# More lead in a shared FFN, spread weight loads, and a scatter that waits for its own transfers

## The reference

```python
scores = sigmoid(h @ gate_w.T)                 # 32 experts in 4 groups
topi   = top 8 of the 2 best groups            # per token
x_lat  = h @ fc1_w.T                           # 512 -> 256
y_lat  = sum over the 8 of cw * (relu(x_lat @ w1[e].T)**2 @ w2[e].T)
shared = relu(h @ shared_up_w.T)**2 @ shared_down_w.T    # 512 -> 1024 -> 512
out    = x + shared + y_lat @ fc2_w.T
```

## Time and profile before

| | us |
|---|---|
| median of 3 runs (lowest, highest) | 1316.29 (1312.57, 1317.66) |
| the profiled execution, its own time | 1316.76 |
| its span | 1314.9 |
| PE busy in the span | 1110.3 (84%) |
| POOL busy in the span | 595.5 (45%) |

### The profile page before, as it was taken

How to read it: one execution, slowest core, us unless ns; L and a number is a source line. 1 busy time by engine, 2 the same in 40 slices (tenths; PEclk the granted TensorE clock), 3 DMA queues, 4 the chain that set the end, 5 groups by cost and what they waited for, 6 DMA issues and landing times.

```text
span 1314.9 us, 14151 instructions
## 1 busy us (share of the span) xinstructions
PE 1110.3 (84%) x3686; PEld 651.0 (50%) x3687; DVE 735.5 (56%) x1387; ACT 461.2 (35%) x694; POOL 595.5 (45%) x461
## 2 busy tenths in 40 slices
PE   0374499997989899799899589996999999999928
PEld 0131244433433344354444234445888888888813
DVE  8574478989998999751683000003444444444425
ACT  3352256535653655241211011111333333333400
POOL 3223204641464147400037666621777777777720
PEclk9987799998999899899899789997999999999959
DMA  3969901002100201301108542236777777777684
GB/s 129 303 209 357 368 5 48 25 16 72 48 24 16 80 8 32 115 0 64 64 36 279 189 164 94 90 121 201 131 121 133 124 127 129 123 132 122 86 237 171
DMA packets 125731, 157.57 MB, mean 120 GB/s; under 512 B 8705, under 2 KB 103937, under 8 KB 125697
## 3 DMA queue, kind: packets, MB, share of 16 engines
q1 hardware_dynamic: 96512, 117.83, 29.2%
q0 software_dynamic: 29184, 39.34, 16.1%
HBM read 79.67 MB, written 77.46 MB: 120 GB/s over the span
## 4 chain that ended last, share of the span: by engine, by line
PE 55%; DVE 19%; another core or an unknown queue 6%; issue 6%; DMA 5%; SPq 4%; ACT 2%; POOL 1%; DVEq 0%; POOLq 0%; ACTq 0%
PE banks L561 11%; PE banks L582 11%; PE banks L490 8%; PE banks L1556 8%; PE banks L513 6%; DMA arena<-fT 4%; DVE arena L1336 3%; DVE arena L1433 3%; PE banks L551 3%; PE banks L572 3%; PE banks L1574 2%; PE banks L473 2%; DVE arena L1317 2%; DVE arena L1344 1%
## 5 line engine op out<-in xcount | busy, mean ns | idle before, releaser
L1556 PE MATMUL banks<-arena 128*128 128x512 f32 x896 | 390.4, 596 | 28.7 <-ACT arena L1092 18.9
L451 POOL DMA_INDIRECT sums<-arena x160 | 249.6, 1560 | 142.8 <-ACT arena L688 112.1
L1556 PEld LDWEIGHTS banks<-arena 128*128 128x128 f32 x896 | 171.3, 191 | 245.6 <-issue 225.3
L439 POOL DMA_INDIRECT slots_in<-arena x128 | 129.3, 1010 | 106.3 <-issue 86.4
L490 PE MATMUL banks<-arena 128*128 128x512 f32 x320 | 148.5, 611 | 16.2 <-ACT arena L659 13.3
L561 PE MATMUL banks<-arena 128*128 x640 | 153.0, 382 | 0.0
L582 PE MATMUL banks<-arena 128*128 x640 | 151.2, 379 | 0.0
L513 PE MATMUL banks<-arena 128*128 128x512 f32 x256 | 118.8, 608 | 8.8 <-DVE arena L894 7.1
L1574 PE MATMUL banks<-arena 128*128 128x512 f32 (+1 forms) x64 | 44.3, 856 | 96.7 <-DVE arena L1399 72.6
L561 PEld LDWEIGHTS banks<-arena 128*128 128x128 f32 x640 | 116.5, 192 | 13.2 <-issue 0.4
L843 DVE SCALAR_TENSOR_TENSOR arena<-arena 128x256 f32<-128x256 f32 x160 | 72.1, 490 | 89.2 <-ACT arena L673 89.2
(11 more groups left out here) (179 smaller groups left out, 1367.2 us busy)
## 6 DMA issues: line engine op xcount, KB each, us to landing
slots_in<-arena SPq DMA_DIRECT2D x8, 2800.0 KB, 18.4
arena<-slots_in SPq DMA_DIRECT2D x80, 280.0 KB, 3.3
sums<-arena SPq DMA_DIRECT2D x4, 2176.0 KB, 20.5
arena<-fT SPq DMA_DIRECT2D x32, 256.0 KB, 2.6
arena<-xT SPq DMA_DIRECT2D x8, 1024.0 KB, 5.5
arena<-w2T SPq DMA_DIRECT2D x4, 2048.0 KB
arena<-sums SPq DMA_DIRECT2D x16, 512.0 KB, 8.7
arena<-w1T SPq DMA_DIRECT2D x3, 2048.0 KB
```

The source lines that it names most:

```text
L439: pool.indirect_dma_start(rows_in, bass.IndirectOffsetOnAxis(ap=POSU[:, n, j:j + 1], axis=0), XLR[:, n], None).then_inc(S['scattered'], 16)
L451: pool.indirect_dma_start(sums[g % RING], bass.IndirectOffsetOnAxis(ap=DESTU[:, g:g + 1], axis=0), YO[:, i % 4, c], None, compute_op=ALU.add)\
L1556: ins = pe.matmul(out, w[:, k, m * P:(m + 1) * P], x[:, k], start=(k == 0), stop=(k == kt - 1))
```

## The change

Three edits go together.

- **Lead.** LAG = KS - 2 = 6: PE does `up(0)` to `up(5)`, `ranks()`, and then `up(n)`, `down(n-6)` alternately; at the end six `down` tiles stand together.
- **Gate and fc1 tiles.** AHEAD = EARLY - 3 = 9: tiles 9, 10 and 11 move from ahead of `k2` to behind `v2`, with banks 5, 6 and 3. Their logits and rows move behind the last sequence's sigmoid and `XS` on ACT and DVE. Waits on `rows_copied` and `logits_copied` move with them.
- **Loads and scatter.** W2's four quarters and the first three of W1 are issued one by one between `up_mm` 16 and 32. `xg_load` of the first four pairs now stands ahead of the last four W1 loads (its buffer is moved, so that it doesn't lie over `HS`), behind a wait for all of `scattered`. POOL drops the waits for `up_mm` and waits instead, after every second token tile (16 DMAs), until all issued so far have landed. PE's wait for W1 and W2 moves behind the first two transposes of the experts.

```diff
-            for e in range(0, E, quarter):
-                sp.dma_start(W2[:, e:e + quarter], w2[:, e:e + quarter]).then_inc(S['w2_loaded'], 16)
+            load_w2(0)
             sp.wait_ge(S['up_mm'], KS * 2)
-            load_w1(0)
+            load_w1(0, quarter)
+            load_w2(1)
+            sp.wait_ge(S['up_mm'], KS * 2 + KS // 2)
+            load_w2(2)
+            sp.wait_ge(S['up_mm'], KS * 3)
+            load_w1(quarter, quarter // 2)
+            load_w2(3)
             sp.wait_ge(S['up_mm'], KS * B)
-            load_w1(1)
-            load_w1(2)
+            load_w1(quarter + quarter // 2, quarter // 2)
+            load_w1(2 * quarter, quarter)
+            sp.wait_ge(S['scattered'], 16 * NT * TOPK)
+            for i in range(4):
+                xg_load(sp, i, i, 0)
             for k in range(0, KS, 2):
...
-            sp.wait_ge(S['scattered'], 16 * NT * TOPK)
-            for i in range(4):
-                xg_load(sp, i, i, 0)
...
                 for j in range(TOPK):
-                    g = (n * TOPK + j) // 4
-                    if j % 4 == 0:
-                        pool.wait_ge(S['up_mm'], 5 + 3 * g // 4)
                     pool.indirect_dma_start(rows_in, bass.IndirectOffsetOnAxis(ap=POSU[:, n, j:j + 1], axis=0),
                                             XLR[:, n], None).then_inc(S['scattered'], 16)
-            pool.wait_ge(S['scattered'], 16 * TOPK * NT)
+                if n % 2:
+                    pool.wait_ge(S['scattered'], 16 * TOPK * (n + 1))
...
+        LAG = KS - 2
+        def stream():
+            for n in range(KS * B + LAG):
+                if n < KS * B:
+                    yield 'up', n
+                if n >= LAG:
+                    yield 'down', n - LAG
...
+        AHEAD = EARLY - 3
+        FG_BANK = [(3, 4, 0, 1, 7, 2)[n % 6] if n < AHEAD else (5, 6, 3, 4, 7, 2, 5)[n - AHEAD] for n in range(NT)]
...
+                if n == AHEAD:
+                    pe.wait_ge(S['r2_evac'], 4 * B)
+                if n == NT - 1:
+                    pe.wait_ge(S['rows_copied'], AHEAD + 1)
+                    pe.wait_ge(S['logits_copied'], AHEAD + 1)
...
-            fg_tiles(pe, range(3, EARLY))
+            fg_tiles(pe, range(3, AHEAD))
...
-            pe.wait_ge(S['w1_loaded'], 16 * (3 + KS // 2))
-            pe.wait_ge(S['w2_loaded'], 64)
             pe.wait_ge(S['routed'], 2)
             pe.wait_ge(S['down_evac'], K * B)
             pe.wait_ge(S['up_relu'], KS * B)
             t1(0, 0, 0)
             t1(1, 1, 0)
+            pe.wait_ge(S['w1_loaded'], 16 * (4 + KS // 2))
+            pe.wait_ge(S['w2_loaded'], 64)
             m1(0, 0, 0, experts(0))
```

More of the change, by code:

```diff
@@ L321, in build @@
         assert top[0] <= hs_end
+        YO = place(4, 2, LAT)
+        assert top[0] >= hs_end
         XGB = place(4, 2, ROW)
-        YO = place(4, 2, LAT)
         assert top[0] <= rings_end
@@ L368, in part2_sp, with load_w2, load_w1 @@
             quarter = E // 4
-            def load_w1(n):
-                sp.dma_start(W1[:, n * quarter:(n + 1) * quarter], w1[:, n * quarter:(n + 1) * quarter])\
-                  .then_inc(S['w1_loaded'], 16)
             sp.wait_ge(S['routed'], 2)
             ld(sp, FC2, 'fc2T').then_inc(S['fc2_loaded'], 16)
-            for e in range(0, E, quarter):
-                sp.dma_start(W2[:, e:e + quarter], w2[:, e:e + quarter]).then_inc(S['w2_loaded'], 16)
-            sp.wait_ge(S['up_mm'], KS * 2)
-            load_w1(0)
-            sp.wait_ge(S['up_mm'], KS * B)
-            load_w1(1)
-            load_w1(2)
+            def load_w2(n):
+                sp.dma_start(W2[:, n * quarter:(n + 1) * quarter], w2[:, n * quarter:(n + 1) * quarter])\
+                  .then_inc(S['w2_loaded'], 16)
+            def load_w1(e, n):
+                sp.dma_start(W1[:, e:e + n], w1[:, e:e + n]).then_inc(S['w1_loaded'], 16)
+            load_w2(0)
+            sp.wait_ge(S['up_mm'], KS * 2)
+            load_w1(0, quarter)
[5 more added lines that the diff above has]
+            load_w2(3)
+            sp.wait_ge(S['up_mm'], KS * B)
+            load_w1(quarter + quarter // 2, quarter // 2)
[3 more added lines that the diff above has]
+                xg_load(sp, i, i, 0)
             for k in range(0, KS, 2):
@@ L387, in part2_sp @@
                     sp.wait_ge(S['down_mm'], K * B)
-                sp.dma_start(W1[:, E - KS + k:E - KS + k + 2], w1[:, E - KS + k:E - KS + k + 2]).then_inc(S['w1_loaded'], 16)
-            sp.wait_ge(S['scattered'], 16 * NT * TOPK)
-            for i in range(4):
-                xg_load(sp, i, i, 0)
+                load_w1(E - KS + k, 2)
             with sp.Fori(0, NP // 4 - 1) as h:
@@ L455, in build @@
         DOWN_BANK = (2, 3, 4, 7)
+        LAG = KS - 2
[5 more added lines that the diff above has]
+                    yield 'down', n - LAG
         EARLY = NT - TT
-        FG_BANK = [(3, 4, 0, 1, 7, 2)[n % 6] if n < EARLY else (5, 6, 7, 2)[n - EARLY] for n in range(NT)]
+        AHEAD = EARLY - 3
+        FG_BANK = [(3, 4, 0, 1, 7, 2)[n % 6] if n < AHEAD else (5, 6, 3, 4, 7, 2, 5)[n - AHEAD] for n in range(NT)]
         def fg_tiles(pe, tiles):
@@ L468, in fg_tiles @@
                     pe.wait_ge(S['v2_evac'], 4 * B)
-                if 6 <= n < EARLY:
+                if 6 <= n < AHEAD:
                     pe.wait_ge(S['rows_copied'], n - 5)
                     pe.wait_ge(S['logits_copied'], n - 5)
+                if n == AHEAD:
[3 more added lines that the diff above has]
+                    pe.wait_ge(S['logits_copied'], AHEAD + 1)
                 for k in range(K):
@@ L518, in down @@
                     ins.then_inc(S['down_step'], 1)
-            fg_tiles(pe, range(EARLY, NT))
+            fg_tiles(pe, range(AHEAD, NT))
             def ranks():
@@ L527, in ranks @@
                   .then_inc(S['ranked'], 1)
-            for n in range(KS * B + 2):
-                if n < KS * B:
+            for of, n in stream():
+                if of == 'up':
                     up(n)
[L532 to L536, removed]
+                else:
+                    if n == 0:
+                        pe.wait_ge(S['rows_copied'], NT)
+                    down(n)
+                if of == 'up' and n == 5:
                     ranks()
@@ L716, in did @@
                 step.wait()
-            rows(dve, range(EARLY, NT))
+            rows(dve, range(AHEAD, NT))
             front_done(dve)
@@ L1244, in _ @@
             own(2, B - 1)
-            logits(act, range(6, EARLY))
+            logits(act, range(6, AHEAD))
             for m in range(K):
@@ L1250, in _ @@
             sig_new(B - 1)
+            logits(act, range(AHEAD, EARLY))
             part2_act(act, step)
@@ L1543, in _ @@
             rows(dve, range(0, 6))
-            mixes(2, B - 1, between=lambda n: rows(dve, range(6 + 3 * n, 9 + 3 * n)))
+            mixes(2, B - 1, between=lambda n: rows(dve, range(6 + 3 * n, min(9 + 3 * n, AHEAD))))
             for m in range(K):
@@ L1618, in k2 @@
                 for m in range(K):
-                    if last:
-                        pe.wait_ge(S['rows_copied'], EARLY - 5 + m)
-                        pe.wait_ge(S['logits_copied'], EARLY - 5 + m)
+                    if last and m < 3:
+                        pe.wait_ge(S['rows_copied'], AHEAD - 2 + m)
+                        pe.wait_ge(S['logits_copied'], AHEAD - 2 + m)
                     if not last:
@@ L1630, in r2 @@
                         pe.wait_ge(S['k2_evac'], 4 * b + m - 1)
[L1631 to L1634, removed]
+                    elif not (isinstance(b, int) and b == B - 1):
                         pe.wait_ge(S['v_evac'], 4 * b + 7 + m)
```

## The result

The changed kernel took 1296.61 us (median of four runs, 1295.81 to 1303.36) beside 1316.62 us for the kernel before: ratio 0.9865, 95% interval 0.9826 to 0.9904. That is 20 us and not the 36 us of the forecast. It lies inside the range and 15.6 us above the point.

A forecast was written before the change was run, and what follows sets the result against it. The shared FFN, from 638.1 to the experts' first W1 product at 901.99, was taken as the bound. Scatter landed at 855 plus 10.8 us of loads gives 866, a 36 us shift: 1316.8 - 36 = 1280.8, so 1281 us; range 1271 to 1298.

The forecast's parts named there:

- Front: Gate tiles ahead of the shared FFN: PE's 5.83 us gap filled, next tile at the upper clock; 7.9 us gained.
- Lead: `down` six tiles behind `up` in the shared FFN: costs nothing, helps where `down` waits for the square.
- Scatter: POOL's scatter: waits for PE, 20.7 us, go; seven landing waits add 17 us; last issue at 853, landed at 855.
- Loads: Behind the last scatter: 3.24 MB of slots and W1 take 10.8 us; first W1 product at 866.
- PE's cover: End of the shared FFN: PE ends at 851.6 with some 11 us to spare; smaller late increments cost nothing.
- signs of being wrong: Waits for L659 or L894 of 20 us and more, PE's last `down` after 875, or scatter ending beyond 865.
- rival in which PE ends last: Shared FFN: increments stay late, PE loses the same 29.5 us and ends at 881; 1299 us, chance 0.14.

The follow-up runs named there:

- 1288 group: The five comparisons, of changed kernels against the kernel before, in which the kernel before had a median of 1287.5 to 1289.1 us.
- after_third: The changed kernel run again without an edit, against the kernel before: 1295.60 us beside 1288.48 us, ratio 1.0056.
- 1316 group: The forecast's comparison and one later one, in which the kernel before had medians of 1316.6 and 1315.7 us.
- after_again: The changed kernel run again without an edit, against the kernel before: 1327.05 us beside 1315.74 us, ratio 0.9921.
- no_pacing_again: The changed kernel with a single landing wait behind all 128 scatters, run a second time: 1386.77 us beside 1315.74 us for the kernel before, ratio 1.0542.

## Why the prediction was wrong in size

**Front, right.** The gap is gone and the tile behind it is at the upper clock; the FFN started at 629.7 (630.2 forecast), the scatter at 668.8 (669.2). Alone it is worth 8.2 us in time (7.9 forecast). That the starts fit to half a microsecond is partly luck: in the other traces with this front the FFN starts between 629.8 and 633.4.

**Lead, right.** It changes nothing on PE. Its worth is that of the loads issued earlier, 6.4 us in the 1288 group, which the forecast had inside the step on the loads.

**Scatter, a term too small.** I took 17 us more than the usual distance for seven landing waits. Measured in the forecast's comparison: 22.6 us of waits, less 7 x 0.3 us that lie between any two, 20.5 us; in the 1288 group 26.5 us of waits, so 24.4 us. In the quiet a wait cost 1.5 us more than the usual distance (1.2 forecast), under load 4.1 to 5.8 us (4 forecast), inside the bounds; one more fell under the loads behind the last `up` in the 1288 group. I also missed a stop of 3.3 us ahead of the 114th scatter (2.9 to 6.2 us), which every kernel has there and which I had counted with the waits for PE that would go. The last scatter's landing took 2.46 us in after_third, from the start of its issue. The Trainium skill (DMA: Bandwidth & Descriptors, Anatomy of one DMA) gives an estimate of 2.3 us for it; the trace agrees.

**Loads, 2.6 us short.** From the last landing at 867.7 to the first product at 881.06 it was 13.4 us in the 1288 group, 10.8 forecast. Together, as an estimate: even without late increments the first product would have come at 859.3 + 15.8 = 875 in the forecast's comparison, 9 us behind the 866 that I gave.

**PE's cover, the step that failed.** I wrote that PE has 11 us to spare and that a pause after every 16 scatters would keep late increments below that, since the stretch from 749.07 had gone 12 scatters without one. PE lost 25.5 us, ended at 876.7 and set the start: 876.66 + 4.6 = 881.26 (3.5 us was the forecast for what follows PE's end). One of the signs of being wrong, a last `down` later than 875, was met. The rival in which PE ends last gave 881 for PE's end and 1299 us for the time; it is what happened there. I had its mechanism only by half. I read the late ReLUs as increments on their way, and argued with slack. The run without pacing shows PE itself held to one matmul in 2.8 us while POOL scatters, and four banks of slack gave back 4 of 114 us. The 15.6 us of the miss are then 9 us of scatter and loads, which late increments hid, and 6 us more of PE. That the time lies inside the range is partly luck: of the ten later executions of the same kernel in the 1316 group nine took 1309 us and more, above the 1298 us where the range ends.

**What the landing waits are worth.** Two answers. In the 1316 group, under the profiler, pacing of some kind is needed: without any, PE lost 114 us, with landing waits 25.5 and 56.3 us in the two traces of the changed kernel. In the 1288 group they cost 22 us (1295.60 against 1273.54 us with the waits for PE, in one comparison) and turn a change worth 16 us into a loss of 7. So the same landing waits stand in a kernel that gained 20 us in the one comparison and lost 7 us in the other.

The Trainium skill (SBUF — State Buffer, SBUF: two separate sides) says that transfers and compute don't slow each other on the SBUF's ports. The run without pacing agrees with it in the 1288 group (106 matmuls in 44.8 us). The 16 matmuls of the 1316 group speak against it only if the hold lies in those ports, which no run shows.

**Open.** What holds PE, and why in one group and not in the other; whether it does so at all when no trace is taken. Whether the length of a pause decides. The forecast's trace speaks for it (the late increments begin behind a pause of 1.76 us and not behind the three of 4.4 to 5.9 us), two others against (the first late one of after_again came behind 5.89 us, and the stop of 3.31 us freed nothing in no_pacing_again); the three runs with longer pauses fell into the other group. Whether the waits for PE serve better than landing waits in the 1316 group: that kernel, 1272.2 to 1274.3 us in four comparisons of the 1288 group and as fast there as the one without pacing, has not run in it. It keeps POOL from running ahead of a PE that is held, as the kernel before does, where that cost 28 to 30 us.

## What to carry to other kernels

A gap whose releaser is no engine, in one trace, may belong to the conditions of that comparison: repeat the comparison before designing around it, and count whether the trace holds all the increments that the program makes. Ask of every wait that paces one engine whether it binds when all goes well; here a wait on the progress of the engine that suffers cost nothing then, and waits on one's own landings cost 22 us. And when two chains end close together (here PE at 852 + 5 and the scatter at 853 + 13), work out both, for the one that looks covered decides as soon as its cover is spent.

## What the runs showed of the hardware that I had not expected

- The same program takes 1288 us in five comparisons and 1316 us in two, one of each under the same chip number, and without pacing 1272 and 1387 us.
- While POOL issued indirect transfers 1.275 us apart, PE did one 128x512 matmul in 2.8 us in the 1316 group, at a granted clock of 0.58 over that window, with the DMA share at 0.31; the trace kept 375 of the scatter's 2,048 increments. The adds of the experts' stage, the two of a pair 1.86 us apart, did not hold PE there: 315.00 of 315 us busy in this window of the changed kernel, forecast's comparison.

```profile
900.00:1215.00 315.00, 315.00 (x1746) 277.87 (x1746) 149.77 (x511) 122.25 (x218) 226.84 (x146) 1.00 0.75 125
```

- POOL stops for 3.3 us (6.16 us in after_again) between its 113th and 114th scatter in every kernel, whenever that falls (821 to 869), for no wait of the program. In the changed kernel PE was free again behind it, without pacing it was not.
